# Moving DRAM clears, expert loads, the router and the last tile's steps to other places of a written-out order, and laying the first batch's keys in two halves

## What is computed

```python
x = x + tanh(g_xattn) * attention(layernorm(x), ctx, ctx)      # 16 heads, Wq, Wk, Wv, Wo with biases
xt = layernorm(x).reshape(896, 256)
idx = argmax(softmax(xt @ wg))                                 # 8 experts
locations = cumsum(one_hot(idx), axis=0) - one_hot(idx)        # place of a token in its expert
kept = locations < 112                                         # capacity of an expert
x = x + tanh(g_ffn) * gate * kept * (xt @ W[idx].T + b[idx])
```

## Time and profile before

| | us |
|---|---|
| median of 3 runs | 209.12 |
| lowest and highest run | 206.82, 212.23 |
| the profiled execution, its own time | 210.57 |
| span of the profiled execution | 208.7 |
| PE busy | 182.5 (87%) |
| DVE, ACT, POOL busy | 125.8, 97.2, 94.6 |

### The profile page before, as it was taken

The page is one execution under the profiler, slowest core; times in us unless marked ns, Lnnn a source line. Parts: engine busy times, 40 slices in busy tenths (PEclk is TensorE's granted clock), DMA queues, the critical chain, the costliest instruction groups (busy, mean ns, idle before and its releaser), DMA issues.

```text
span 208.7 us, 4473 instructions
## 1 busy us (share of the span) xinstructions
PE 182.5 (87%) x1723; PEld 107.1 (51%) x1723; DVE 125.8 (60%) x301; ACT 97.2 (47%) x215; POOL 94.6 (45%) x159
## 2 busy tenths in 40 slices
PE   0775879699999959999999999998997987989992
PEld 0443744456456535656646656555555544446741
DVE  6476368765485536548558657668815305588842
ACT  4656147345565553457457368366555353013200
POOL 6587554861290581059157356533050680102750
PEclk9999589999999996999999999999998596999999
DMA  5969953487159999505904910903330234900210
GB/s 135 292 155 214 238 134 97 117 221 161 39 156 214 297 250 204 133 16 154 224 10 122 227 52 4 219 5 121 97 102 0 91 121 115 276 21 24 76 57 22
DMA packets 18733, 27.20 MB, mean 130 GB/s; under 512 B 3872, under 2 KB 13449, under 8 KB 18600
## 3 DMA queue, kind: packets, MB, share of 16 engines
q1 hardware_dynamic: 16117, 23.65, 45.8%
q0 software_dynamic: 864, 2.07, 3.2%
q10 hardware_dynamic: 1731, 1.20, 2.1%
HBM read 10.03 MB, written 5.06 MB: 72 GB/s over the span
## 4 chain that ended last, share of the span: by engine, by line
PE 67%; DVE 7%; DMA 7%; SPq 5%; ACT 4%; POOL 3%; issue 3%; ACTq 1%; DVEq 0%; POOLq 0%
PE pv L524 12%; PE stp L508 12%; PE sc L496 9%; PE pj L446 4%; PE stp L432 3%; PE pj L612 3%; PE misc L559 3%; PE pj L468 3%; PE pj L451 3%; DVE nmax L945 2%; DMA q<-parts_q 2%; DMA wk_sb<-in_wk 2%; SPq L393 2%; DMA q<-mrows 2%; PE pj L473 2%
## 5 line engine op out<-in xcount | busy, mean ns | idle before, releaser
L945 DVE TENSOR_REDUCE nmax<-sc 112x1 f32<-112x375 f32 x128 | 67.2, 544 | 41.9 <-PE sc L496 41.0
L852 ACT ACTIVATE prob<-stp 128x448 f32<-128x448 f32 (+1 forms) x96 | 52.2, 544 | 55.2 <-PE stp L508 54.3
L496 PE MATMUL sc<-k,q 128*112 128x375 bf16 x128 | 41.2, 346 | 6.5 <-DMA q<-parts_q 3.0
L524 PE MATMUL pv<-prob,v_sb 128*32 128x112 f32 (+1 forms) x768 | 39.7, 281 | 2.3 <-issue 1.5
L508 PE MATMUL stp<-q,k 128*128 128x112 bf16 x384 | 36.7, 220 | 2.3 <-DMA q<-mrows 2.3
L508 PEld LDWEIGHTS stp<-q,k 128*128 128x128 bf16 x384 | 21.2, 100 | 19.6 <-issue 16.9
L524 PEld LDWEIGHTS pv<-prob,v_sb 128*32 128x32 f32 (+1 forms) x768 | 15.8, 111 | 23.9 <-issue 14.9
L496 PEld LDWEIGHTS sc<-k,q 128*112 128x112 bf16 x128 | 16.3, 133 | 15.5 <-DVE nmax L945 9.5
L1205 POOL CAST mparts<-nmax 112x16 bf16<-112x16 f32 x8 | 1.6, 196 | 45.1 <-DVE nmax L945 45.1
L446 PE MATMUL pj<-ctx_sb,wk_sb 128*128 128x375 f32 x32 | 14.0, 534 | 7.0 <-DMA wk_sb<-in_wk 6.5
L1189 POOL TENSOR_TENSOR kf<-kf,parts_k 128x375 f32<-128x375 f32 x14 | 12.6, 897 | 11.6 <-ACT kf L751 11.5
(11 more groups left out here) (150 smaller groups left out, 261.5 us busy)
## 6 DMA issues: line engine op xcount, KB each, us to landing
k<-parts_k SPq DMA_DIRECT2D x48, 187.5 KB, 3.8
ctx_sb<-in_ctx SPq DMA_DIRECT2D x8, 375.0 KB, 4.3
early<-in_wT SPq DMA_DIRECT2D x8, 256.0 KB, 4.7
slots<-empty SPq DMA_DIRECT2D x8, 224.9 KB, 4.2
ctx_sb<-slots SPq DMA_DIRECT2D x8, 224.9 KB, 4.4
q<-parts_q SPq DMA_DIRECT2D x12, 112.0 KB, 2.7
q<-parts_q SPq DMA_DIRECT2D x6, 168.0 KB, 4.3
k<-in_be SPq DMA_DIRECT2D x1, 896.0 KB, 5.0
```

The source lines that it names most:

```text
L496: pe.matmul(sc[h % 2][0:NQ, 0:NK], q_heads(b)[:, h, :], k6_flat[:, b % KR, h * NK:(h + 1) * NK], start=True, stop=True).then_inc(s_sc, 1)
L524: mm = pe.matmul(pv[32 * j:32 * j + 32, g * NQ:(g + 1) * NQ], v_sb[0:kn, b % VR, v_block(c, 4 * g + j), :], prob[0:kn, n % 3, j * NQ:(j + ...
L852: nc.scalar.activation(prob[0:kn, n % 3, :], stp[n % 2][0:kn, 0:4 * NQ], ACT.Exp, scale=SCALE).then_inc(s_p, 1)
L945: nc.vector.tensor_reduce(nmax[:, b % 2, h:h + 1], sc[h % 2][0:NQ, 0:NK], axis=AX.X, op=ALU.max, negate=True).then_inc(s_max, 1)
```

## The change

1. **First loads.** The first context is loaded in two pieces (rows 0 to 127 of its width, and the rest), and so are the key weights. The weights' pieces are the first DMAs on ACT's queue; batch 0's x moves from ACT's queue to SP's, between the two context pieces. `project_k(0, n)` waits for the pieces one by one.
2. **First keys in halves.** `lay_first_k(m)` lays half m alone, with 6 DMAs of 128 runs of 375 elements, and is called for m = 0, then the first queries' last part, then m = 1. Batch 0's scores take the even heads first (`head_of`).
3. **Clears and experts.** The 8 clears of `slots` at step 30 are now 4 at step 42 and 4 at step 54. The expert loads move from steps 32, 44, 56, 68 to 55, 67, 79, 91.
4. **Router of batches 0 to 5.** `route` moves from step 101 to 104, `places` from 102 to 105, `assign` from 102 to 106; the scatters from 102, 103, 104, 108, 109, 110 to 108 to 113. Batch 7's bias is added to x at step 100, not 106. Batch 6's `turn_xn2` and `logits` come a step earlier each (110, 111).
5. **Behind the loop.** In PE's stream the third dense product of batch 6 comes ahead of `turn_xn2(7)`, the bias and `logits(7)`, and the first `turn_xin` behind `places(2)`; DVE adds the first dense products before the bias.

```diff
-XBO_AT = 22
+XBO_AT = (22, 34, 46, 58, 70, 82, 94, 100)
+CLEAR_AT, EXPERTS_AT = (42, 54), (55, 67, 79, 91)
-ROUTE0_AT, PLACE0_AT, ASSIGN0_AT = 101, 102, 102
-SCAT_AT = (102, 103, 104, 108, 109, 110)
-LN6_AT = 107
+ROUTE0_AT, PLACE0_AT, ASSIGN0_AT = 104, 105, 106
+SCAT_AT = (108, 109, 110, 111, 112, 113)
+LN6_AT, X2T6_AT, LG6_AT = 107, 110, 111
...
+def head_of(b, n):
+    return (2 * n if n < H // 2 else 2 * n - H + 1) if b == 0 else n
...
+            def lay_first_k(m):
+                for part, ready in ((0, s_khi), (1, s_kmid), (2, s_klo)):
+                    sp.wait_ge(ready, m + 1)
+                    for j in range(len(K_PART)):
+                        if K_PART[j] == part:
+                            sp.dma_start(k6_flat[j:128:STEP, 0, 0:H * NK]
+                                         .rearrange("p (h m n) -> p h m n", m=2, n=NK)[:, :, m, :],
+                                         parts_k[:, 0, part, m, :]).then_inc(s_k0laid[m], 16)
...
-            load_ctx(0)
+            sp.dma_start(ctx_sb[:, 0, 0, :], ctx[:, 0, 0, :]).then_inc(s_ctx0[0], 16)
+            sp.dma_start(x_sb[:, 0, :], x[:, 0, :]).then_inc(s_x[0], 16)
+            sp.dma_start(ctx_sb[:, 0, 1, :], ctx[:, 0, 1, :]).then_inc(s_ctx0[1], 16)
...
-            lay_k(0)
+            sp.wait_ge(s_kones[0], 1)
+            lay_first_k(0)
             lay_q(0, parts=(2,))
+            lay_first_k(1)
             load_ctx(2)
...
-                if s == 30:
+                if s in CLEAR_AT:
                     sp.wait_ge(s_empty, 1)
-                    for e in range(E):
+                    for e in range(4 * CLEAR_AT.index(s), 4 * CLEAR_AT.index(s) + 4):
...
-                if s in (32, 44, 56, 68):
-                    for e in range((s - 32) // 6, (s - 32) // 6 + 2):
+                if s in EXPERTS_AT:
+                    for e in range(2 * EXPERTS_AT.index(s), 2 * EXPERTS_AT.index(s) + 2):
...
             def project_k(b, n):
-                if n == 0:
+                if b == 0 and n != 1:
+                    pe.wait_ge(s_ctx0[n // 2], 16)
+                    pe.wait_ge(s_wk[n // 2], 16)
+                if b > 0 and n == 0:
                     pe.wait_ge(s_ctx[b], 16)
...
             dense(0, 1)
+            dense(0, 2)
+            turn_xn2(B - 1)
             choose_bias(0)
-            turn_xn2(B - 1)
+            logits(B - 1)
+            dense(0, 3)
+            places(2, B - 1, B)
             turn_xin(0)
-            logits(B - 1)
-            dense(0, 2)
-            places(2, B - 1, B)
-            dense(0, 3)
             turn_xin(1)
...
-            act.dma_start(x_sb[:, 0, :], x[:, 0, :]).then_inc(s_x[0], 16)
+            for n in range(2):
+                act.dma_start(wk_sb[:, n, :], wk[:, n, :]).then_inc(s_wk[n], 16)
             act.dma_start(bqkv_sb[:, :], bqkv).then_inc(s_bias, 16)
-            act.dma_start(wk_sb[:, :, :], wk).then_inc(s_wk, 16)
...
             add_x(B - 1)
+            add_dense(0, 0)
             normalise_2(B - 1)
+            add_dense(0, 1)
             take_bias(0)
-            add_dense(0, 0)
+            add_dense(0, 2)
             route(2, B - 1, B)
-            add_dense(0, 1)
             weigh(1)
-            add_dense(0, 2)
             add_dense(0, 3)
```

More of the change, by code:

```diff
@@ L207, in build @@
         s_bo = sem("bo_loaded")
-        s_wk = sem("wk_loaded")
+        s_wk = [sem(f"wk_{n}_loaded") for n in ("rows_0_to_127", "rest")]
         s_wq = sem("wq_loaded")
@@ L215, in build @@
         s_be8 = sem("expert_bias_rows_loaded")
+        s_ctx0 = [sem(f"ctx_0_{n}_loaded") for n in ("rows_0_to_127", "rest")]
         s_ctx = [sem(f"ctx_{b}_loaded") for b in range(B)]
@@ L247, in build @@
         s_klo = sem("k_lo_ready")
+        s_k0laid = [sem(f"{n}_heads_of_first_k_laid") for n in ("even", "odd")]
         s_klaid = [sem(f"k_rows_laid_{i}") for i in range(2)]
@@ L692, in _ @@
                     turn_bv()
-                if found := at(s, X2T_AT, 1):
+                if (found := at(s, X2T_AT, 1)) and found[0] < GATHERED:
                     turn_xn2(found[0])
-                if found := at(s, LG_AT, 1):
+                if (found := at(s, LG_AT, 1)) and found[0] < GATHERED:
                     logits(found[0])
+                if s == X2T6_AT:
+                    turn_xn2(GATHERED)
+                if s == LG6_AT:
+                    logits(GATHERED)
                 if s == PLACE0_AT:
@@ L742, in k_hi @@
                 act.wait_ge(s_k, 2 * b + m + 1)
-                if b >= 2 and m == 0:
-                    act.wait_ge(s_klaid[b % 2], 16 * len(K_PART) * (b // 2))
+                if b == 2 and m == 0:
+                    for half_laid in s_k0laid:
+                        act.wait_ge(half_laid, 16 * len(K_PART))
+                if b > 2 and m == 0:
+                    act.wait_ge(s_klaid[b % 2], 16 * len(K_PART) * ((b - 1) // 2))
                 nc.scalar.activation(parts_k[:, b % 2, 0, m, :], pj[m][:, 0:NK], ACT.Identity,
@@ L879, in _ @@
                            .then_inc(s_mrow, 16)
-                if found := at(s, X2T_AT, 1):
+                if (found := at(s, X2T_AT, 1)) and found[0] < GATHERED:
                     leave_x2T(found[0])
-                if found := at(s, LG_AT, 1):
+                if (found := at(s, LG_AT, 1)) and found[0] < GATHERED:
                     leave_logits(found[0])
+                if s == X2T6_AT:
+                    leave_x2T(GATHERED)
+                if s == LG6_AT:
+                    leave_logits(GATHERED)
                 if s == ROUTE0_AT:
@@ L1042, in take_bias @@
                 nc.vector.tensor_tensor(last[:, t, :], (stp, sc)[t][1][0:NQ, 0:D],
-                                        rows[:, GATHERED + t, X1:X1 + D], ALU.add).then_inc(s_beTe, 1)
+                                        (last[:, t, :], rows[:, GATHERED + t, X1:X1 + D])[t], ALU.add)\
+                    .then_inc(s_beTe, 1)
                 dve.wait_ge(s_beTe, t + 1)
@@ L1048, in add_dense @@
                 dve.wait_ge(s_dense, 4 * t + p + 1)
+                so_far = last[:, t, :] if t or p else rows[:, GATHERED, X1:X1 + D]
                 link(nc.vector.scalar_tensor_tensor(last[:, t, :], bank[0:NQ, 0:D], share[:, t, 2 * p:2 * p + 1],
-                                                    last[:, t, :], ALU.mult, ALU.add))
+                                                    so_far, ALU.mult, ALU.add))
                 second = bank[0:NQ, D:2 * D]
@@ L1280, in _ @@
                     more_constants()
[L1281 to L1282 removed]
+                if s in XBO_AT:
+                    b = XBO_AT.index(s)
                     pool.wait_ge(s_tbo, 1)
```

35 lines of the change are left out of this document (18 added, 17 removed).

## The result

The kernel before had a median of 209.59 us in 20 runs, the changed kernel 204.68 us (lowest 201.78). The ratio is 0.9749, with a 95% interval of 0.9708 to 0.9789: 2.5% faster, where 5.3% was predicted. Ratios leave disturbed runs out and medians do not, so the two can differ by 1%.

The account below looks back on a forecast made before the run. Undisturbed turns were taken as PE-bound, leaving waits and low clock to win. Terms A to E sum to -11.75, from the profiled 210.57 to 198.8, then 198.1 us toward the median; the 8-in-10 range was 194 to 203.5.

Parts of the forecast that it names:

- A: At the first score: split key weights and halved first keys let queries land sooner; -2.2 us, between -1.0 and -3.0.
- B: Behind the first score: less low clock from 20 to 27 us after a shorter PE wait; -1.2 us, between 0 and -2.4.
- C: The 20.58 us turn: batch 2's max rows no longer queue behind SP's clears and expert loads; -3.9 us.
- D: Steps 102 to 113: later router lets batch 6's turn_pv go first, ending the loop sooner; -3.85 us, between -1.5 and -5.4.
- E: Behind the loop: first dense product no longer at low clock, PE almost without pause; -0.6 us, between +1.0 and -1.5.
- from the profile to the median: Whole kernel: profiled execution was 1.45 us above the median; half of that taken off, 198.8 to 198.1 us.
- the halves bring nothing: Rival at the start: packets cost the same at 750 B, so A is 0.5 and B 0; 201.0 us, chance 0.13.
- the clock falls all the same: Rival: remaining gaps still lower the clock, so B is 0 and D and E lose 2.1; 201.4 us, chance 0.20.
- the mixtures of two rivals: Two rivals occurring together, near 204 to 206 us; chance 0.04.
- Stalls of the turns with clears: Rival: the long turn's stall moves to one of the two turns with clears; 202.0 us, chance 0.08.
- late experts' rows: Rival behind the loop: with all scatters in a row, experts' rows come late, 2.5 us lost; 200.6 us, chance 0.03.
- the slower case: Rival: SP's queue falls behind in every turn given clears or experts, four turns wait; 213.8 us, chance 0.02.

Follow-up runs that it names:

- e5: The changed kernel run again unaltered, on chip B, beside the kernel before: 205.63 us, ratio 0.978.
- e9: The changed kernel run a third time unaltered, on chip C, beside the kernel before: 199.49 us, ratio 0.971.
- e6: The changed kernel with parts 1 and 2 undone (start as in the kernel before), on chip B: 205.33 us.
- e12: The changed kernel with first keys laid whole and heads in usual order, loads still in pieces, on chip C: 196.83 us, ratio 0.956 to the kernel before.
- e2: The changed kernel with the eight clears and the expert loads back at their old steps, on chip A: 204.71 us, ratio 0.984 to the kernel before.
- e3: The changed kernel with router, batch 6's transposes and logits, scatters and the last addition to x at old steps, chip A: 202.49 us, ratio 0.972 to the kernel before.
- e14: The changed kernel run again unaltered, on chip D, beside the kernel before: 205.85 us, ratio 0.983.
- e7: The changed kernel with first keys whole and batch 1's keys and group 1's queries laid in mixed order, chip B: 203.32 us, ratio 0.968 to the kernel before.
- e4: The changed kernel with first keys laid whole and heads in usual order, loads still in pieces, on chip A: 197.40 us, ratio 0.939 to the kernel before.

## Why the prediction was wrong

Forecast and result are 198.1 and 204.68, and the range ended at 203.5. In the profiled execution the terms came out thus:

| term | forecast | measured |
|---|---|---|
| A + B, to the maxima of batch 1 | -3.4 | -2.6 |
| C, the long turn | -3.9 | -3.9 |
| D, to the loop's last context product | -3.85 | -4.1 |
| E, behind the loop | -0.6 | +1.9 |
| sum | -11.75 | -8.8 |
| from the profile to the median | -0.7 | +2.9 |

**A** came out at the size forecast, 2.4 us at the first score, ended by ACT as its floor had it, but in part by luck. The queries' last part took 2.0 us to landing instead of 5.09 and landed at 17.34, four us sooner and not 2.5, so the halves gained 3.1 us in the queue, close to the 3.0 that the prediction set aside, and ACT's floor took back what was too much. With pieces and whole keys the first score came at 20.0 to 20.2 in three of four profiles, so the pieces gave some 1.2 us (0.5 forecast) and the halves 1.1 (2.0 forecast).

**The step that failed in A and B** is "so it is covered by the scores of the even heads", with the sentence behind it on the third context. They look at the next reader of each: the ninth score for the odd half, the projection 10 us on for the context. For these they hold. But the transfers put off by the odd half's six issues share the DMA engines with batch 1's lays, and this term stood at nothing. The pause moved from the first score to batch 1's first, 1.9 us, and low clock is found from 38 to 41 us instead of 20 to 27 (from 33 to 36 and 40 to 43 in e5 and e9). In three more profiles of the changed kernel A + B is 0.5 to 0.7 us, not 2.6, and e6 beside e5 puts it at nothing. In those profiles nearly 3 of the 3.4 us are missing; in the first profile, from which the table is made, 0.8. The rival "the halves bring nothing" gave them 1.7 + 1.2 less, for another reason, and none had them cost something, as e12 beside e9 shows (2.7 us).

**C** was right in mechanism and size. e2 adds that its worth depends on the rest: 3.9 us beside the old start, 6.6 us with the other edits in.

**D** was right in mechanism: 4.1 us in the first profile, with late signals in both kernels, and by e3, without any, 3.0 us in the loop and 1.0 behind it, against 3.85.

**E failed by its sign.** The step is "PE works here almost without a pause, in either order": PE stood 1.33 us before `through_wo` of batch 7, and ran at half clock from 164.2 to 167.6. The cause stood in D: "I can't say whether this comes back", of the exp that stood 1.60 us. It was priced at half, as a chance event. It belongs to the chip and the scatters, and the change may have given it more to act on: all six scatters now fall where PE hands its last groups to ACT and DVE. The exp stood 2.04 us, and turn_pv, which had no such wait before, 3.06 us; then the clock fell. Where no signal is late, D and E together take 55.2 - 48.2 = 7.0 us off the stretch from the last turn of maxima to the end (rest of the program included), against 4.45 forecast, though the profile of before has late signals in its share. Where signals are late, three profiles of the changed kernel have 53.0, 54.8 and 55.2: 2.2, 0.4 and 0.0 us less than before.

**The median.** I took 0.7 us off because the profile of before was above its median. The changed kernel's profile was the lowest of its 20 runs, so 2.9 us go the other way, and the term is the largest miss of the sum, 3.6 of 6.6 us. Other runs have more low clock: e5 and e14 have 6.8 us instead of 3.4 in the first place where it falls, and 10.2 instead of 3.4 in the second. The forecast thus fits a chip without late signals best: there, on C, the change brought 207.86 - 199.49 = 8.4 us by the medians and 6.0 by the ratio, still short of the 11.0 forecast; on B and D 4.3 and 4.0 by the medians, 4.6 and 3.5 by the ratios.

**The rivals.** Of those that occurred "the clock falls all the same" (201.4) comes nearest: it fell, but at new places and behind new waits. The result itself lies among the mixtures of two rivals, 204 to 206, which had a chance of 0.04. Stalls of the turns with clears, late experts' rows and the slower case did not occur.

**A version that beats both** came of the experiments: the changed kernel with the first keys whole. It had 0.939, 0.956 and 0.946 of the kernel before on A, C and E, 2.7 us below the changed kernel on C (its four fastest runs of six, 195.7 to 197.5, are below all of e9's). On a chip with late signals it ran only with mixed lays (e7: 0.968, beside 0.978 of the changed kernel).

## What to carry to other kernels

A transfer taken off a wait is not yet free: list all that stands behind it in the same queues, and ask when each next reader needs it and which transfers it will then share the engines with. Splitting a transfer in two doubles its issues: here six more held back the next load by 3.6 us, while the engines were half idle, and the wait moved to the next group. An idle time whose releaser had long been done is a term of its own, to be priced whole both ways, and a second chip tells more of it than more runs on the first.

## What the runs showed of the hardware

- PE's completion signals can arrive 0.4 to 3.3 us late while GpSimd's scatters run or have just gone out, in both first profiles and on chips B and D, and not on A, C and E. Without the scatters none is late, on A, C and D. ACT's and DVE's signals were not late in either first profile. Which of queue and bytes does it was not told apart.
- DVE's normalisations of 112 x 256 took 0.41 us alone, 2.23 us for two that began 1.7 us before GpSimd's memsets ended, and 3.77 us for two with both memsets beside them. The Trainium skill, "SBUF — State Buffer", section "SBUF: two separate sides", has GpSimd and a DVE operation in a two-port mode share one port pair, which the one that starts first keeps for its whole instruction while the other stands still. By that rule the trace agrees in the length: 3.77 - 2 x 0.41 = 2.95 us is the length of the memsets (1.62 + 1.37 = 2.99). In the order it adds something: DVE's second normalisation began at 14.99, before the memsets at 15.26 but beside GpSimd's instruction of 14.88 to 15.32, and ended 0.15 us behind the last memset, so GpSimd's instructions that followed without a gap went ahead of it.
- Packets of 750 bytes between on-chip tiles took 49 ns in the changed kernel and 45 in e9, those of 1500 bytes 114 ns in e12, at 12 to 21 us.
- The granted clock was low (1.2 GHz, against 2.4) for 3 to 10 us between 32 and 45 us in every profile with halves, in six of them within 1.3 us of the end of a pause of 1.8 to 2.0 us and in six 5 to 6 us behind one of 1.9 to 2.6 us, beside a second one of 1.0 to 1.2 us. It stayed up all through e4 and e12, whose pauses of 1.4 and 1.7 us ended at 20 us, and one of 0.99 us at 37.8 and 37.9. In e7 a pause of 1.9 us that ended at 20 us was followed by a low clock, from 21.5 to 24.2.
